# Two graph layers in one block, with the end of the first layer interleaved among its last sums

## The reference

```python
h = relu(layernorm(x)); x = x + L0(h, src, dst)      # attention, 4 heads of 32
h = relu(layernorm(x)); x = x + L1(h, src, dst, edge_attr, edge_weight)

# L0: t = h @ W + b; logits = leaky_relu(sum(concat(t[src], t[dst]).reshape(-1,4,64) * alpha))
#     att = softmax of the logits over the edges of a receiver; out = sum of att * t[src] + bias
# L1: ef = (relu(ea @ We1 + be1) @ We2 + be2) * sigmoid(ts @ Wt + bt)
#     msg = relu(concat(h[src], ef) @ Wn1 + bn1) @ Wn2 + bn2
#     out = sum over the edges of a receiver of msg, + h
```

## Time and profile before

| | us |
|---|---|
| median of 3 runs | 2123.77 (2120.2 to 2126.13) |
| the profiled execution | 2122.82, span 2121.0 |
| busy in the span: PE / DVE / ACT / POOL | 1524.8 / 1461.3 / 929.9 / 1563.2 |
| gathers of the first layer, L356 | 764 x 0.951 |
| gathers of the second layer, L1044 | 812 x 0.949 |

### The profile page before, as it was taken

One profiled execution on the slowest core, in us unless ns is written; L12 is line 12 of the kernel. 1 busy time (PEld: TensorE's weight loads), 2 busy tenths in 40 slices (PEclk: granted clock), 3 DMA queues, 4 the chain that ended last, 5 costly groups with the idle time before them and its releaser, 6 DMA issues.

```text
span 2121.0 us, 47035 instructions
## 1 busy us (share of the span) xinstructions
PE 1524.8 (72%) x8785; PEld 1051.5 (50%) x8785; DVE 1461.3 (69%) x5237; ACT 929.9 (44%) x2818; POOL 1563.2 (74%) x1660
## 2 busy tenths in 40 slices
PE   6556555555555454454658998989989898898888
PEld 5434444444444343343545665656555555555556
DVE  8676767676766566565786886777767676666667
ACT  8535253535353342442466444444434443444343
POOL 7777777777777777777277777777777777777775
PEclk9766666666666666566679999999989999999999
DMA  7222222222222222222063544545544444454453
GB/s 203 54 57 57 57 57 57 58 57 57 57 58 57 56 58 57 57 56 54 22 184 107 144 144 144 145 123 146 150 128 144 144 145 144 119 146 138 133 151 105
DMA packets 111001, 213.56 MB, mean 101 GB/s; under 512 B 35214, under 2 KB 74350, under 8 KB 100723
## 3 DMA queue, kind: packets, MB, share of 16 engines
q0 software_dynamic: 51968, 107.32, 19.1%
q1 hardware_dynamic: 53031, 101.47, 16.2%
q10 hardware_dynamic: 5708, 1.77, 0.4%
HBM read 197.54 MB, written 12.88 MB: 99 GB/s over the span
## 4 chain that ended last, share of the span: by engine, by line
POOL 26%; issue 11%; PE 6%; DVE 5%; DMA 2%; ACT 1%; DVEq 1%; ACTq 0%; POOLq 0%; SPq 0%
POOL acc L1044 26%; DMA acc<-table,index 2%; PE pair L1122 1%; DVE acc L1392 1%; PE bank L1131 1%; PE pair L1116 1%; PE bank L1142 1%; DVE onehot L1350 1%; DVE pre L1374 1%; DVE ef L1357 1%; DVE x_rows L1288 0%; ACTq L1239 0%; PE bank L1073 0%; ACT msg L1223 0%; ACT hidden L1210 0%
## 5 line engine op out<-in xcount | busy, mean ns | idle before, releaser
L1044 POOL DMA_INDIRECT acc<-table,index x812 | 770.2, 949 | 252.5 <-issue 242.3
L356 POOL DMA_INDIRECT rows<-table,index x764 | 726.5, 951 | 233.0 <-issue 228.4
L812 ACT ACTIVATE rows<-rows,edge_w 128x32 f32<-128x32 f32 x1626 | 351.9, 313 | 1.1 <-issue 0.4
L504 DVE TENSOR_TENSOR acc<-acc,pair 128x256 f32 x832 | 349.2, 420 | 3.9 <-issue 2.5
L499 DVE TENSOR_SCALAR onehot<-iota_row,dst_rel 128x128 f32<-128x128 f32 x832 | 252.0, 304 | 135.2 <-PE pair L675 103.8
L1392 DVE TENSOR_TENSOR acc<-acc,bank 128x128 f32 x832 | 239.0, 287 | 143.5 <-issue 35.7
L675 PE MATMUL pair<-onehot,rows 128*128 128x128 f32 x1626 | 334.2, 367 | 0.5 <-ACT rows L812 0.5
L675 PEld LDWEIGHTS pair<-onehot,rows 128*128 128x128 f32 x1626 | 285.7, 264 | 58.9 <-issue 30.3
L1210 ACT ACTIVATE hidden<-pair,be 128x512 f32<-128x512 f32 x208 | 142.9, 687 | 380.0 <-PE pair L1122 172.4
L1131 PEld LDWEIGHTS bank<-wn1b,ef 128*128 128x128 f32 x1664 | 232.1, 202 | 109.7 <-issue 104.0
L1116 PE MATMUL pair<-ea,we 64*128 64x512 f32 x416 | 243.9, 668 | 42.4 <-DMA ea<-in_ea_t 42.4
(11 more groups left out here) (168 smaller groups left out, 1207.9 us busy)
## 6 DMA issues: line engine op xcount, KB each, us to landing
ts<-in_ts SPq DMA_DIRECT2D x52, 1024.0 KB
rows_x<-table SPq DMA_DIRECT2D x1664, 0.5 KB
ea<-in_ea_t SPq DMA_DIRECT2D x52, 512.0 KB, 5.0
rows_y<-table SPq DMA_DIRECT2D x1664, 0.5 KB
acc<-table,index POOLq DMA_INDIRECT x812
moments<-table ACTq DMA_DIRECT2D x768, 0.5 KB
rows_z<-table ACTq DMA_DIRECT2D x768, 0.5 KB
rows<-table,index POOLq DMA_INDIRECT x764
```

The lines of the kernel that those rows point to most:

```text
L356: gp.indirect_dma_start(rows0[:, n % (RING * TG), :], None, table1, bass.IndirectOffsetOnAxis(index[:, n:n + 1], 0)).then_inc(half_in[g % ...
L504: dve.tensor_tensor(acc2[:, :, ds(v, P)], acc2[:, :, ds(v, P)], both_sums[n // TG % 2][:, :, n % TG * P:(n % TG + 1) * P], ALU.add).then_i ...
L812: act.activation(row, row, ACT.Copy, scale=edge_w[:, r % 2, (g - SPANS[r][0]) * TG + t, h:h + 1]).then_inc(scaled0, 1)
L1044: gp.indirect_dma_start(rows[:, g % RG1, t, :], None, table, bass.IndirectOffsetOnAxis(index[:, n:n + 1], 0)).then_inc(gathered[g % RG1], 16)
```

## The change

1. The two blocks become one: every engine runs its first list and then its second without the barrier (`first_vector(dve)`, `second_vector(dve)` and so on).
2. The 13 units are now cut at `CUTS`, so that a unit is closed by one group: 2 blocks, then 4 eleven times, then 3. `turn_stats` and `gather_stats` of units 0 to 8 stand among the groups of the last but one turn (`CLOSE`), and the denominators are computed for these nine units before the last four groups and for the other four units after them.
3. `scaled_sums` of units 0 to 4 and `mix` of units 0 and 1 stand among the last four groups on VectorE. `mix` of units 2 to 8 moves to GpSimd (`GP_MIXES`); VectorE keeps 0, 1 and 9 to 12. `part` has four slots instead of two. GpSimd's own terms are split in a product and an add, in an order that puts a product ahead of each add.
4. TensorE's turns of statistics and sums use banks 6 and 7, later 7, 5 and 6; the small matrices of the maxima move to bank 5. `turn_penalties` stands after the second group of a turn instead of the first, `keep_row_penalties` after the third, and the parts of the last turn's maxima one group earlier.
5. SP stores `table3` first, in 13 stores that follow the units, and issues the weights and edge data of the second layer behind them.
6. Tile 830, which holds 10 edges, is no longer gathered by GpSimd: SP fetches its 10 rows one by one, in both layers (763 and 811 gathers are left).

The diff without indentation, cut to its core. In this order: VectorE's list (a turn, the last but one turn, the last turn and what follows it), `scaled_sums` on VectorE, `mix` as GpSimd has it for units 2 to 8, GpSimd's wait before its first gather, SyncE's list with the rows of tile 830 and the stores of new x.

```diff
-            if k == 1:
+            if k == 2:
                 keep_row_penalties(r)
...
+    for k, g in enumerate(groups(CLOSE)):
+        if k == HALF:
+            at = first_of(g)
+        sum_group(g, at[k % HALF * TG:(k % HALF + 1) * TG])
...
+        if k >= 1:
+            gather_stats(k - 1)
+    at = first_of(g1)
+    gather_stats(7)
+    gather_stats(8)
+    maxima_of(0)
+    dve.wait_ge(acc0, g1 * TG)
+    rescale(LAST, at)
+    shares(0)
+    sum_group(g1, at[0:TG])
+    scaled_sums(0)
+    sum_group(g1 + 1, at[TG:2 * TG])
+    scaled_sums(1)
+    mix(0)
...
+    add(n + 3, at[3 * TG + 3])
+    gather_stats(12)
+    maxima_of(1)
+    scaled_sums(5)
+    shares(1)
+    scaled_sums(6)
+    scaled_sums(7)
+    scaled_sums(8)
+    scaled_sums(9)
+    mix(9)
+    scaled_sums(10)
+    mix(10)
+    scaled_sums(11)
+    mix(11)
+    scaled_sums(12)
+    mix(12)
...
+    def scaled_sums(u):
+        dve.wait_ge(ca_ready, stage_of(u) + 1)
+        dve.wait_ge(s_t, u + 1)
+        if u >= PART_SLOTS:
+            wait_mixed(dve, u - PART_SLOTS)
...
+    def mix(u):
+        gp.wait_ge(parted, u + 1)
+        gp.wait_ge(own, u + 1)
+        gp.tensor_tensor(x_rows[:, blocks_of(u), :], x_rows[:, blocks_of(u), :], part[:, u % PART_SLOTS, 0:spread_of(u)],
+                         ALU.add).then_inc(gp_mixed, 1)
...
-    gp.wait_ge(x1_out, 16 * UNITS)
+    gp.wait_ge(x1_out, 16 * PARTS)
...
+    sp.wait_ge(agg0, SHORT // TG - RING + 1)
+    for o in range(0, E % P, BATCH):
...
+            sp.dma_start(rows0[o + q:o + q + 1, SHORT % (RING * TG), :], table1[ds(row, 1), :]).then_inc(tail_in, 16)
     sp.wait_ge(w2_in, 32)
+    for u in range(PARTS):
+        wait_mixed(sp, u)
+        sp.dma_start(table3[CUTS[u] * P:CUTS[u + 1] * P, :].rearrange("(b p) c -> p b c", p=P), x_rows[:, blocks_of(u), :]).then_inc(x1_out, 16)
```

More of the change, by code:

```diff
@@ L44 @@
 RAW_TURNS = 2
+WCOL = 4 * SH * (RT + 2)
+CARRY = WCOL + 2 * SH * (RT + 2)
 RAW = sum(SPAN_SIZES[:RAW_TURNS]) * TG
@@ L59 @@
 ACT_TILES0 = [SPANS[r][0] * TG + 1 for r in range(ACT_TURNS + 2, TURNS, ACT_TURNS)]
-EMPTY = range(-(-E // P), TILES)
+SHORT = E // P
+EMPTY = range(SHORT, TILES)
 BATCH = 16
@@ L66 @@
 assert all(0 < y - x <= TG for x, y in zip(CUTS, CUTS[1:]))
+LAST, CLOSE = TURNS - 1, TURNS - 2
+STAGES = [0, SPANS[LAST][0] - FIRST_END, PARTS]
+assert STAGES == [0, 9, 13] and SPANS[CLOSE][1] == RG
+PART_SLOTS = 4
+GP_MIXES = range(2, STAGES[1])
 ACT_ROWS = 4
@@ L123, in gnn_layers @@
             rows0 = sb("rows0", [P, RING * TG, RW], st=st)
+            spare = rows0[:, GROUPS % RING * TG:RING * TG, :].rearrange("p t c -> p (t c)")
+            spare_after = GROUPS - GROUPS % RING
+            sums_t, top, den = (spare[:, o * NB:(o + m) * NB].rearrange("p (b c) -> p b c", b=NB) for o, m in ((0, LCOL + SH), (8, HEADS), (12, HEADS)))
+            parts = spare[:, 16 * NB:24 * NB].rearrange("p (k b c) -> p k b c", k=2, b=NB)
+            part = spare[:, 24 * NB:24 * NB + PART_SLOTS * TG * CH].rearrange("p (k m c) -> p k m c", k=PART_SLOTS, c=CH)
+            own_scale, sum_scale = parts[:, 1], parts[:, 0]
             rows_x = sb("rows_x", [P, LINE_SLOTS, RW], st=st)
-            line_index = sb("line_index", [1, len(LINE_TILES) * P], i32, st)
+            line_index = sb("line_index", [1, (len(LINE_TILES) + 1) * P], i32, st)
             bias_all = sb("bias_all", [P, CH], st=st)
@@ L848, in _ @@
                             keep_logits(r + 1)
+                    fetch(r)
+                    if r < CLOSE:
+                        keep_logits(r + 1)
+                shares_up(1)
         with ExitStack() as st:
[L852 to L855 removed]
             bn1_all = sb("bn1_all", [P, CH], st=st)
             wn1a = sb("wn1a", [P, CH], st=st)
[L858 removed]
@@ new lines, in second_gpsimd, with gather @@
+            def second_gpsimd(gp):
+                def gather(g, table):
+                    for t in range(TG):
+                        n = g * TG + t
+                        if n not in LINE_TILES1 and n not in ACT_TILES and n not in EMPTY:
+                            gp.indirect_dma_start(rows[:, g % RG1, t, :], None, table,
+                                                  bass.IndirectOffsetOnAxis(index[:, n:n + 1], 0)).then_inc(gathered[g % RG1], 16)
+                gp.wait_ge(x1_out, 16 * PARTS)
+                for g in range(RAW1):
+                    gather(g, table3)
+                for q in range(PROJ_SLOTS):
+                    gp.wait_ge(table1_out[q], 16 * len(range(q, UNITS, PROJ_SLOTS)))
+                for g in range(RAW1, GROUPS):
+                    if g >= RG1:
+                        gp.wait_ge(radd, g - RG1 + 1)
+                    gather(g, table2)
@@ new lines, in gnn_layers, with _ @@
+        with nc.Block() as block:
+            @block.gpsimd
+            def _(gp):
+                first_gpsimd(gp)
+                second_gpsimd(gp)
+            @block.scalar
+            def _(act):
+                first_scalar(act)
+                second_scalar(act)
+            @block.sync
+            def _(sp):
+                first_sync(sp)
+                second_sync(sp)
+            @block.tensor
+            def _(pe):
+                first_tensor(pe)
+                second_tensor(pe)
+            @block.vector
+            def _(dve):
+                first_vector(dve)
+                second_vector(dve)
```

1906 lines of the change are left out of this document (983 added, 923 removed).

## The result

The changed kernel takes 2117.99 us in the median of 8 runs (2114.61 to 2119.9), the kernel before 2121.26 us in 8 runs beside it (2120.2 to 2126.13). The ratio is 0.9978, with a 95% interval of 0.9968 to 0.9988: 4.7 us less by it, between 2.5 and 6.8, and 3.3 by the two medians. The forecast was 2118.0. The profiled executions stand at 2119.36 (span 2117.6) and 2122.82 (span 2121.0), 3.46 apart. The runs of one kernel are spread over 5 us, so a single profile says where a microsecond went inside the program, and little about the median.

A forecast was written before the change was run, and what follows sets the result against it. GpSimd's gapless second-layer gathers were taken as the bound: 4.9 (earlier start) + 1.25 (one gather less) - 0.3 (waits) = 5.8 us off 2122.82, 2117.0, so median 2118.0; 8-in-10 range 2113.5 to 2125.

The forecast's parts named there:

- What bounds: Second layer: GpSimd's gathers run without a gap, 1.254 us apart; when they start and how many there are set its length.
- M: Time when VectorE's last mix between the layers ends: 1086.87 before, forecast 1082.0, with the first gather 2.6 later.
- The closing turn and the first shares: End of the first layer: turn's end left at 1043.1, scales ready at 1049.4, sum of unit 2 at 1057.0.
- GpSimd's mix: Between the layers: seven 128x512 adds moved to GpSimd, taken at 1.3 us each, 9.1 for all seven.
- The bounds of 1.0 and 2.3: Lowest and highest time in us that the forecast considered for one 128x512 add on GpSimd.
- the meeting at the port: Between the layers: three VectorE mixes of 0.7 come in GpSimd's way at the shared SBUF port, 2.1 us.
- The loads behind the stores: Second layer's start: statistics wait for bias and `wn1a`, begin at M + 4.3; `table2` complete 38.8 after first gather at most.
- The charge of 0.3: Second layer: 0.3 us in all for GpSimd's waits for `table2` (1.3 to spare) and for `radd`.
- signs of being wrong: Wrong if VectorE never waits for GpSimd, GpSimd stops over 1 us at `table2` or `radd`, or first-layer gathers show gaps.
- the loads come due: Rival: M holds, but stores to `table2` queue behind 3 MB, conversion 2 to 4 us late; 2120 to 2122; chance 0.08.
- One gather less: Tile 830 leaves GpSimd's queue: 1.25 us off the end of the second layer, nothing taken for the first.
- The sum: 4.9 + 1.25 - 0.3 = 5.8 us off the profiled 2122.82 gives 2117.0; the median, 0.95 above, 2118.0.

## Why the prediction was right in its number, and where its steps failed

*What bounds.* Right up to the last 50 us: the gathers are a row without gaps, and the first one starts at M + 2.34 (forecast 2.6).

*The closing turn and the first shares.* The turn's last add ended at 1042.99 (1043.1), the scales were ready at 1048.2 (1049.4). GpSimd waits from 2.91 us before 1056.39, where 1057.0 was forecast. The three agree within 1.2 us. The last group's adds ended at 1062.1 (1064).

*GpSimd's mix.* 1.26 to 1.28 against 1.3, own adds 0.72 to 0.73. The bounds of 1.0 and 2.3 were wide, and the choice of 1.3 held; from the own add to this one it is 2.1 ns per element, not 1.8. "GPSIMD Engine Reference" of the Trainium skill, section "3.1 Elementwise — side-by-side cycle accounting", gives 2.6 cycles per element, an estimate of 1.1 us before a fixed part; the measured 1.27 agrees. The last own add ended at 1078.8 (1080.1), M came at 1080.4 (1082.0), the first gather at 1082.76 (1084.6): 1.8 us better than forecast, with GpSimd the bound, as said.

*What the forecast had not priced.* It charged the meeting at the port to GpSimd and let VectorE off. The rows have VectorE's operations stretched by up to 1.1 us, small ones included. "SBUF — State Buffer" of the Trainium skill, section "SBUF: two separate sides", gives the exclusive lock not only to VectorE's operations with two SBUF inputs but also to those in what it calls a 2-port perf mode, and counts a float32 copy from SBUF to SBUF among them. The trace agrees with both: the mixes and the 60-column product have two SBUF inputs, the 15-column copy, 1.25 us instead of 0.17, has one. The change's gain between the layers would have been 2.3 larger without the very move to GpSimd.

*The loads behind the stores.* The statistics began at M + 4.1 (M + 4.3). The charge of 0.3 for what that does to GpSimd was wrong: `table2` let GpSimd on at 41.1 us behind the first gather (38.8 at most), and the waits were 1.1 and 0.9 us beyond the usual, 2.0 in sum. A stop of more than 1 us at `table2` or `radd` was one of the forecast's own signs of being wrong. The rival "the loads come due" was a part of what happened.

*One gather less.* Forecast 1.25; it took that off the row of gathers and nothing off the time that can be measured. The failed step is the sentence that what comes behind the last gather is 14.8 us and "unchanged", and with it the premise that the start and the number of the gathers alone set the length of the second layer. The runs showed a chain of products instead: 51.4 to 53.7 us from group 198's `pre` to the end in all twelve profiles that keep TensorE's work, with 14.8 to 63.4 us behind the last gather. In the kernel before the last landing and this chain were level within a microsecond, which a reader of its trace could have seen at the last `pre`; any larger lead of the gathers had to run into that chain.

*The sum.* 6.7 at the start of the gathers (4.9), 1.25 for the gather, 2.0 lost at the two waits (0.3) and 1.0 of pace make 7.0 at the last gather (5.8 was the forecast), and 3.6 lost at the end (0) leave 3.4 in the profile's span. The time forecast was hit closer than the gain: 5.8 us were forecast, 3.3 to 4.7 measured, and the kernel before was itself at 2121.26 in the eight runs, not at the 2123.77 from which the forecast started. That 2118.0 meets 2117.99 is luck: the forecast of the profiled execution, 2117.0, was missed by 2.4 us, and the 2.3 us between a median 0.95 above its profile, as taken, and one 1.37 below it, as measured, cancelled that.

So where the 3.6 went is settled: group 198 led by only 3.8 us, and the chain behind it is as long as before. Why group 198 did not lead by the 7.0 of the gathers is not. In the two profiles 2.7 us of it go between groups 195 and 197, where TensorE ran low for 9 us instead of 4; but that 4 is itself the shortest of all: the kernel before with its last load in pieces, no faster or slower, took 12.9 us from group 194 to 197, the kernel before 11.3, the changed kernel 14.0. No experiment moved this stretch alone: a gather more, pieces for the last load, and less work for TensorE brought no gain that can be told from noise or from the chip. Nor was any part of the change run by itself, so how much the order of the stores and the interleaving each bring at the first gather is not known.

## What to carry to other kernels

When a row of work on one engine is shortened from its front, look at who was level with it at its end: a lead there is worth only the slack that the other chain has. To see which of two chains is the end, measure both to the end of the span over several profiles; here one varied from 14.8 to 63.4 us and the other from 51.4 to 53.7. A wide elementwise operation moved to GpSimd cost VectorE about a microsecond at each operation with all inputs in SBUF that it met here, and nothing at those that read PSUM, so count both engines' lists. And take the chip into account: a program with 3,300 single-row transfers on one queue changes its bound where their issue is slow.

## What the runs showed of the hardware

- While a 128x512 add of two SBUF operands ran on GpSimd (1.27 us), VectorE's 128x512 add took 1.65 to 1.67 instead of 0.68, a 128x60 product 1.12 instead of 0.22, and a copy of 15 columns 1.25 instead of 0.17. Scaled sums of 128x512 with one operand in PSUM kept 0.66 each beside such an add. A GpSimd product of 128x256 beside a 128x128 mask stretched the mask to 0.74 at 1049.61, instead of 0.27 to 0.29.
- TensorE fell from the higher of its two clock levels to the lower one behind idle times of 2.90 and 3.46 us, and stayed there for some 9 us of work (granted clock 0.50); in the kernel before, behind 2.89 us, it began about 1 us later and was low for only about 4 us. Behind 1.55 us it did not fall in the changed kernel, behind 1.89 it did in the run with two loads in pieces. With work taken off it, one idle time grew from 1.55 to 3.46 us, and it ran low behind it.
- On one chip SyncE issued a register-addressed row transfer every 0.74 to 1.29 us, by stretches of 20 us, on another every 0.51, with the same program and the same 0.95 us for a gather on GpSimd.
- The changed kernel stood at 0.9978 of the kernel before in its first runs and at 1.0175 [1.0135, 1.0215] on the chip with the slow row transfers.
